# A four-layer graph network on one core: the second convolution's bias and node factor take another way

## The reference, cut to what matters

```python
def _L2_gnn_ref(H, A, mask, W, b):          # H = relu(layernorm(x)), the second norm of the kernel
    A_hat = A + jnp.eye(N, dtype=A.dtype)
    deg = A_hat.sum(axis=-1)
    dis = (deg + EPS) ** (-0.5)             # the node factor
    A_norm = dis[:, :, None] * A_hat * dis[:, None, :]
    H_lin = jnp.einsum('bni,oi->bno', H, W) + b
    out = jnp.einsum('bnm,bmo->bno', A_norm, H_lin)
    out = out * mask[:, :, None]
    return jax.nn.relu(out)
```

## Time and profile before

| | before |
|---|---|
| time, median of 3 runs (lowest to highest) | 666.03 us (664.73 to 666.15) |
| the profiled execution: its time, its span | 666.43 us, 664.5 us |
| TensorE matmul busy, share of the span | 621.7 us, 94% |
| ScalarE busy | 543.5 us, 82% |
| VectorE busy | 494.7 us, 74% |
| GpSimd busy | 380.8 us, 57% |
| granted TensorE clock, mean | 0.979 of full speed |
| TensorE's share of the chain that ended last | 86% |

### The profile page before, as it was taken

One profiled execution on the slowest core, in us unless ns is written; L12 is line 12 of the kernel. 1 busy time (PEld: TensorE's weight loads), 2 busy tenths in 40 slices (PEclk: granted clock), 3 DMA queues, 4 the chain that ended last, 5 costly groups with the idle time before them and its releaser, 6 DMA issues.

```text
span 664.5 us, 19876 instructions
## 1 busy us (share of the span) xinstructions
PE 621.7 (94%) x7220; PEld 495.6 (75%) x7220; DVE 494.7 (74%) x1530; ACT 543.5 (82%) x1271; POOL 380.8 (57%) x595
## 2 busy tenths in 40 slices
PE   4759999999999999999999999999999999999874
PEld 2545858788696978788696978788696978778563
DVE  4688786887778787878778687878777777975731
ACT  2877779898998989998998989998998889885334
POOL 3277453684847566475846566475846466636321
PEclk9988989999999999999999999999999999999977
DMA  9944590461908255380909154381908244300001
GB/s 117 253 93 134 70 198 3 96 114 31 193 4 157 69 127 98 82 142 27 199 3 164 62 132 94 85 139 31 194 3 150 96 117 41 97 2 18 16 1 33
DMA packets 171628, 61.24 MB, mean 92 GB/s; under 512 B 136641, under 2 KB 155146, under 8 KB 171530
## 3 DMA queue, kind: packets, MB, share of 16 engines
q1 hardware_dynamic: 170898, 59.73, 44.5%
q10 hardware_dynamic: 632, 0.22, 0.2%
HBM read 55.60 MB, written 4.33 MB: 90 GB/s over the span
## 4 chain that ended last, share of the span: by engine, by line
PE 86%; issue 4%; DVE 4%; ACT 2%; POOL 2%; DMA 1%; POOLq 0%; ACTq 0%; DVEq 0%
PE ps L1753 13%; PE ps L1789 9%; PE ps L1802 9%; PE ps L1909 8%; PE ps L1956 8%; PE ps L1739 7%; PE ps L1852 6%; PE ps L1849 5%; PE ps L1850 4%; PE ps L1939 4%; PE ps L1889 3%; PE ps L1695 2%; PE ps L1851 2%; PE ps L1776 1%; PE ps L1923 1%
## 5 line engine op out<-in xcount | busy, mean ns | idle before, releaser
L869 ACT ACTIVATE side<-d_all,sd 128x512 fp8e4<-128x512 f32 x256 | 163.3, 710 | 9.2 <-DVE pos L1302 6.3
L502 POOL TENSOR_TENSOR rstd<-ve,half_neg 128x4 f32<-128x4 f32 (+1 forms) x67 | 73.1, 1092 | 150.1 <-DVE ve L1384 60.7
L1753 PE MATMUL ps<-part,pos 128*128 128x66 bf16 x3072 | 102.5, 193 | 0.0
L1753 PEld LDWEIGHTS ps<-part,pos 128*128 128x128 fp8e4 x3072 | 99.4, 97 | 2.9 <-issue 0.7
L1365 DVE TENSOR_REDUCE best<-ps 128x128 f32<-128x896 f32 x64 | 69.5, 1086 | 27.6 <-PE ps L1853 27.5
L1302 DVE SCALAR_TENSOR_TENSOR pos<-side,edge 128x512 uint32<-128x512 uint32 x64 | 51.1, 798 | 29.0 <-ACT side L869 27.8
L1789 PE MATMUL ps<-adj_tr,h 128*128 128x512 f32 x128 | 60.6, 618 | 1.1 <-ACT h L775 1.1
L1956 PE MATMUL ps<-u,adj_tr 128*128 128x128 f32 x512 | 59.9, 275 | 0.7 <-ACT u L970 0.7
L1956 PEld LDWEIGHTS ps<-u,adj_tr 128*128 128x128 f32 x512 | 58.5, 192 | 1.4 <-ACT u L970 1.4
L1802 PE MATMUL ps<-adj_in,h 128*128 128x512 f32 x128 | 59.4, 608 | 0.0
L1739 PEld LDWEIGHTS ps<-part,edge 128*128 128x128 fp8e4 x1536 | 52.7, 99 | 8.5 <-issue 8.3
(11 more groups left out here) (164 smaller groups left out, 1468.9 us busy)
## 6 DMA issues: line engine op xcount, KB each, us to landing
adj_blk<-in_adj SPq DMA_DIRECT2D x64, 256.0 KB, 7.0
d_all<-d_dram SPq DMA_DIRECT2D x64, 256.0 KB, 5.1
adj_in<-in_adj SPq DMA_DIRECT2D x16, 1024.0 KB, 7.1
x_in<-in_x SPq DMA_DIRECT2D x16, 256.0 KB, 2.9
out_y<-y_out SPq DMA_DIRECT2D x15, 256.0 KB, 6.0
d_dram<-sd_t SPq DMA_DIRECT2D x64, 2.0 KB, 1.5
w_sb<-in_L_gnn_W SPq DMA_DIRECT2D x7, 64.0 KB, 2.1
b_sb<-in_L_gnn_b SPq DMA_DIRECT2D x1, 256.0 KB, 2.6
```

What stands on the lines that cost most here:

```text
L502: G.tensor_tensor(rstd[:, cut], ve[:, cut], half_neg[:, cut], ALU.pow).then_inc(power, 1)
L869: last = A.activation(side[:, t, :], d_all[:, h, :], ACT.Sign, bias=sd[:, 0, h, t:t + 1], scale=-1.0, saturate=False)
L1753: last = mm(ps[:, B_HEADS[q] + i // 2, o:o + VAL], pos[h % 2][:, t, i * P:(i + 1) * P], parts[n][:, t, h, :], start=False, stop=(i % 2 == ...
```

## The change

The bias product `conv_bias` and the making of `b2_rows` are gone. The node factor goes into the norm: VectorE multiplies the variance by the degree before GpSimd takes the power -1/2, so that `rstd2` and the offset hold the factor already and `h2` comes out scaled. `conv_linear` then gives `dis * H W`, and `conv_in`, which is now on VectorE and not on ScalarE, adds `dis * b` on the way out of PSUM. For the largest score, `smax_p` and `smax_t` are now whole: 128 columns and 128 rows, zero outside the 4 that are used, and the transpose and the product go over all 128.

```diff
@@ GpSimd, at the start
+            G.memset(smax_p[:], 0.0).then_inc(s_pool, 1)
+            G.memset(smax_t[:], 0.0).then_inc(s_pool, 1)
@@ GpSimd, degree_sums
                 if g.has(3):
                     pool.wait_ge(deg_ok, g.before(3).all(1))
+                    pool.wait_ge(bn2, g.before(3).all(3))
@@ ScalarE: the piece and its calls are gone
-            @of_graph
-            def conv_in(g):
-                act.wait_ge(lin2_ps, g.halves(1))
-                act.wait_ge(deg_out, g.whole(1))
-                if g.has(2):
-                    act.wait_ge(ay2_ps, g.before(2).all(1))
-                scaled(g, y2[g.two], bank(B_LIN).rearrange("p (t f) -> p t f", t=T), deg_pow[g.three][:, 0, :]).then_inc(y2_ok, 1)
@@ VectorE, top_score
-                V.tensor_reduce(smax_t[:], ps[0:HEADS, B_PROJ, 0:P], AX.X, ALU.min).then_inc(smaxt_ok, 1)
+                V.tensor_reduce(smax_t[0:HEADS, :], ps[0:HEADS, B_PROJ, 0:P], AX.X, ALU.min).then_inc(smaxt_ok, 1)
@@ VectorE, norm2, and the new piece
-                V.tensor_scalar(ve2[:, g.lo:g.hi], mv2[:, g.lo:g.hi, 1], LN_EPS, None, ALU.add).then_inc(bn2, 1)
+                dve.wait_ge(deg_in, g.whole(3))
+                V.scalar_tensor_tensor(ve2[:, g.lo:g.hi], mv2[:, g.lo:g.hi, 1], LN_EPS, deg[g.three][:, 0, g.lo:g.hi],
+                                       ALU.add, ALU.mult).then_inc(bn2, 1)
+            @of_graph
+            def conv_in(g):
+                dve.wait_ge(lin2_ps, g.halves(1))
+                dve.wait_ge(deg_out, g.whole(1))
+                if g.n == 0:
+                    dve.wait_ge(s_w0, 1)
+                if g.has(2):
+                    dve.wait_ge(ay2_ps, g.before(2).all(1))
+                for t in g.tiles:
+                    last = V.scalar_tensor_tensor(y2[g.two][:, t, :], bias_bc[:, 1, :], deg_pow[g.three][:, 0, t:t + 1],
+                                                  bank(B_LIN)[:, t * F:(t + 1) * F], ALU.mult, ALU.add)
+                last.then_inc(y2_ok, 1)
@@ VectorE, the loop (and likewise at the start and the end)
                 pair(1)(at(s - 4))
+                conv_in(at(s - 5))
                 attention(at(s - 4))
                 residual0(at(s - 4))
@@ TensorE
-                tr(ps[0:HEADS, B_PROJ, 0:P], smax_p[:], ident[:]).then_inc(smaxp_ps, 1)
+                tr(ps[:, B_PROJ, 0:P], smax_p[:], ident[:]).then_inc(smaxp_ps, 1)
...
-                mm(ps[:, B_PROJ + 1, 0:HEADS], smax_t[:, 0:1].broadcast_to([HEADS, P]), ident[0:HEADS, 0:HEADS],
+                mm(ps[:, B_PROJ + 1, 0:HEADS], smax_t[:, 0:1].broadcast_to([P, P]), ident[:, 0:HEADS],
                    start=True, stop=True).then_inc(smax_ps, 1)
...
             @of_graph
-            def conv_bias(g):
...
-                mm(bank(B_LIN), ones_b[:], b2_rows[:].unsqueeze(1).broadcast_to([P, T, F]), start=True, stop=False,
-                   skip_group_check=True)
...
             def conv_linear(g):
                 pe.wait_ge(h2t_sb, g.all(1))
...
+                if not g.later:
+                    if g.n >= 1:
+                        pe.wait_ge(u3_ok, g.before(1).halves(1))
+                        pe.wait_ge(z3_ok, g.before(1).halves(1))
+                    else:
+                        pe.wait_ge(best_ok, g.th(3, T))
                 for t in g.tiles:
-                    last = mm(bank(B_LIN)[:, t * F:(t + 1) * F], h2t[:, t * P:(t + 1) * P], w2_t[:], start=False,
-                              stop=(t == T - 1), skip_group_check=True)
+                    last = mm(bank(B_LIN)[:, t * F:(t + 1) * F], h2t[:, t * P:(t + 1) * P], w2_t[:], start=True, stop=True)
```

More of the change, by code:

```diff
@@ L121, in graph_kernel @@
         c6_bc = sb("c6_bc", [P, F])
-        b2_left = sb("b2_left", [P, F])
-        b2_parts = sb("b2_parts", [P, PARTS, F], bf16)
-        b2_rows = sb("b2_rows", [P, F], bf16)
         gamma_c = sb("gamma_c", [P, 1])
         beta_c = sb("beta_c", [P, 1])
-        ones_b = sb("ones_b", [P, P], bf16)
         b1_sb = sb("b1_sb", [P, T, F])
@@ L171, in graph_kernel @@
         d_all = sb("d_all", [P, HEADS, N])
-        smax_p = sb("smax_p", [P, HEADS])
-        smax_t = sb("smax_t", [HEADS, 1])
+        smax_p = sb("smax_p", [P, P])
+        smax_t = sb("smax_t", [P, 1])
         s_rel = sb("s_rel", [P, T, HEADS])
@@ L260, in graph_kernel @@
         s_units = sem("s_units")
-        s_b2 = sem("s_b2")
         s_w0 = sem("s_w0")
@@ L1031, in _ @@
             hidden0(at(3))
-            conv_in(at(0))
             row_sums(at(2))
@@ L1059, in _ @@
             projected(at(3))
-            conv_in(at(1))
             hidden1(at(2))
@@ L1088, in _ @@
                 projected(at(s - 3))
-                conv_in(at(s - 5))
                 row_sums(at(s - 3))
@@ L1114, in _ @@
             projected(at(15))
-            conv_in(at(13))
             sides(0)(at(15))
@@ L1136, in _ @@
             h2_transposed(at(14))
-            conv_in(at(14))
             hidden1(final(0))
@@ L1153, in _ @@
             h2_transposed(final(1))
-            conv_in(final(0))
-            conv_in(final(1))
             conv_relu(final(0))
@@ L1173, in _ @@
             V = nc.vector
[L1175 to L1190, removed]
             V.memset(ones_row[:], 1.0).then_inc(s_setup, 1)
@@ L1194, in _ @@
             V.memset(shift_c[:], SHIFT)
-            V.memset(ones_b[:], 1.0)
             for i in range(2):
@@ L1253, in scores @@
                 V.transpose(sd_t[:], sd[:].rearrange("p k h t -> p (k h t)")).then_inc(dt_ok, 1)
-                V.tensor_reduce(smax_p[:], sd[:, 0, :, :], AX.X, ALU.min).then_inc(smaxp_ok, 1)
+                if g.n == 0:
+                    dve.wait_ge(s_pool, 5)
+                V.tensor_reduce(smax_p[:, 0:HEADS], sd[:, 0, :, :], AX.X, ALU.min).then_inc(smaxp_ok, 1)
             @of_graph
@@ L1469, in unit_columns @@
                 V.tensor_copy(ident_b[:], ident[:]).then_inc(s_units, 1)
-            def bias_rows():
-                three_rows(bias_bc[:, 1, :], b2_parts, b2_left, b2_rows, s_b2)
             norm0(at(0))
@@ L1502, in _ @@
             edge_marks(at(1))
-            bias_rows()
             part_rest(at(1))
@@ L1517, in _ @@
             pair(1)(at(1))
+            conv_in(at(0))
             scores(at(2))
@@ L1543, in _ @@
             pair(1)(at(2))
+            conv_in(at(1))
             attention(at(2))
@@ L1597, in _ @@
             pair(1)(at(14))
+            conv_in(at(13))
             attention(at(14))
@@ L1622, in _ @@
             pair(1)(at(15))
+            conv_in(at(14))
             attention(final(0))
@@ L1641, in _ @@
             norm2(final(1))
+            conv_in(final(0))
+            conv_in(final(1))
             residual2(final(0))
@@ L1996, in _ @@
             mean_value(at(2))
-            conv_bias(at(0))
             conv_linear(at(0))
@@ L2020, in _ @@
             h2_transposed(at(1))
-            conv_bias(at(1))
             row_sums(at(2))
@@ L2049, in _ @@
             for s in range(7, GRAPHS + DEPTH - 1 - 7):
-                conv_bias(at(s - 5))
                 conv_linear(at(s - 5))
@@ L2075, in _ @@
                 h0_transposed(at(s - 1))
-            conv_bias(at(13))
             conv_linear(at(13))
@@ L2097, in _ @@
             h2_transposed(at(14))
-            conv_bias(at(14))
             conv_linear(at(14))
@@ L2116, in _ @@
             h2_transposed(final(1))
-            conv_bias(at(15))
             conv_linear(final(0))
```

## The result

The changed kernel takes 671.37 us, median of 7 runs (667.41 to 672.29), against 666.03 us (664.4 to 667.67, 7 runs): a ratio of 1.0078, 95% interval 1.0055 to 1.0102. It is slower by 5.3 us, where 4.05 were forecast (670.1 us); the time lies inside the forecast's own range of 668 to 672 us. Its profiled execution took 671.91 us with a span of 670.1, 5.6 more than the span of before, at a mean granted clock of 0.972 (0.979 before).

What follows compares the result with a forecast made beforehand. TensorE was taken to set the pace, other engines costing time only where it waits. Terms 2.2 + 0.75 + 0.8 - 0.2 + 0.6 - 0.1 = +4.05 us gave 670.1 us; own range 668 to 672, 8-in-10 range 665.4 to 673.2.

Steps and rivals of the forecast that it cites:

- The direction and the mechanism: Slower, chance 0.73: conv_in on VectorE waits for conv_linear, delaying the chain to h1 until TensorE waits for it.
- The loop: Eleven passes: h1 comes late to TensorE's transposes, +0.20 us per pass, +2.2 us in all.
- The tile: Largest score's product as a whole tile: -0.18 us per graph where h1 is not waited for.
- h1 comes in time: Rival, chance 0.15: a 0.4 us shorter chain to h1 gives -2 us in the loop; 666 us, no change.
- The bias product, the bias rows, ScalarE's relief: Per graph: removed product and row-making were hidden by waits, and y's earlier finish is used by nobody: gain 0.
- TensorE's relief counts: Rival, chance 0.11: h2t ready 0.4 us earlier at conv_linear, so TensorE's savings count: at most 658 us, half 663.
- Graph 1: At the start, conv_in ahead of the attention delays x and the transposes of h1: +0.75 us.
- it costs more: Rival, chance 0.16: longer start wait lowers TensorE's clock again, and conv_in is held up beside GpSimd's xf: 673 us.
- Graph 2: At the start, rden moves by 1.89 us and h1 ends after TensorE wants it: +0.8 us.
- Graph 14: Near the end, h1 stands behind other ScalarE work, so only the whole tile's gain counts: -0.2 us.
- Graph 15: Near the end, a shift of 1.9 us against h1's slack of 1.3: +0.6 us.
- The very end: Last stretch: the bias product has less cover and y is as quick on VectorE: -0.1 us.

Runs made afterwards that it cites:

- e1: The changed kernel with conv_in one piece later everywhere, behind the attention product and ahead of the residual: 662.59 us, ratio 0.9958 to the kernel before.
- e7: The changed kernel with conv_in behind the attention everywhere and the largest score's small 4-column, 4-row products restored: 666.5 us, ratio 1.001 to the kernel before.
- e8: The changed kernel with conv_in as one 512-column instruction in the same place, using the first tile's node factor for all four: 665.13 us, ratio 0.9988.
- e4: The changed kernel with the largest score's products over 4 columns and 4 rows again: 669.65 us, ratio 1.0071 to the kernel before.
- e3: The kernel before without the bias product, the bias left out of the result and its rows still made: 665.56 us, ratio 1.0009.
- e6: The changed kernel with conv_in moved behind the attention at the start and the end alone: 669.31 us, ratio 1.0051 to the kernel before.
- e5: The changed kernel with conv_in moved behind the attention in the loop alone: 666.03 us, ratio 1.0002 to the kernel before.
- e2: The kernel before with only the largest score's two products over whole tiles: 662.2 us, ratio 0.9948.

## Why the prediction was right, and the terms that were not

*The direction and the mechanism.* The chain was forecast step by step, and each link was found: VectorE idle for 0.86 us (0.8 forecast), the four instructions at 1.12 (1.06), a new wait at h1 and at no other place in the loop, `conv_linear` still waiting for `h2t` (the weight loads for 0.47 us, where 0.5 or more was named). e1, e7 and e8 show that nothing else lengthens the pass. x was forecast 3.29 behind the start of `conv_linear` and came 3.24 behind it; the transposes of h1 8.85, and came 8.81.

*The loop: +1.6 for a forecast of +2.2.* The forecast was 0.20 us per pass, measured 0.15 over 11. The tile, mis-sized with 0.18 instead of 0.28, does not matter here (e4), and would have mattered in every case in which h1 is in time: "h1 comes in time" had -2 for the loop and measures 11 x 0.28 = -3.1 (e1).

*The bias product, the bias rows, ScalarE's relief: 0.* Right: e3 shows it for the product, and e7 for all three together. The rival in which TensorE's relief counts fails at the point that it named: `conv_linear` starts no closer to the transposes ahead of it.

*Graph 1: +1.7 for +0.75.* The mechanism was right: `att` and `x` took 0.69 each and not 1.20 and 1.64. After, VectorE:

```profile
78.85 1.12 DVE L1364 SCALAR_TENSOR_TENSOR y<-bias_bc,deg_pow,ps 128x128 f32<-128x128 f32 x4 [1.07 <-PE ps L1868]
...
80.59 0.69 DVE L1306 TENSOR_TENSOR att<-num,rden 128x512 f32<-128x512 f32 x1
81.31 0.69 DVE L1316 TENSOR_TENSOR x<-att,xf 128x512 f32<-128x512 f32 x1
```

and TensorE, which answers to the earlier trace rows:

```profile
77.66 1.16 PE L1868 MATMUL ps<-w_t,h2t 128*128 128x128 f32 x8 [0.45 <-ACT h2t L923]
...
86.88 1.12 PE L1761 MATMUL ps<-ident,h 128*128 128x128 f32 x4 [2.86 <-ACT h L773]
...
88.08 6.18 PE L1787 MATMUL ps<-adj_in,h 128*128 128x512 f32 x8
```

The transposes start 9.22 us behind `conv_linear` instead of 86.66 - 78.13 = 8.53: +0.69, as forecast. The other 1.0 us is what the prediction had put into its rival "it costs more": the transposes themselves take 1.12 us instead of 0.66 and the product behind them 6.18 instead of 5.40. Three microseconds of that product after (window, its length, then busy time of PE, PEld, DVE, ACT, POOL, granted clock, DMA share, GB/s):

```profile
88.00:91.00 3.00, 3.00 (x6) 1.45 (x6) 2.24 (x8) 2.97 (x9) 0.85 (x1) 0.50 1.18 266
```

The transposes and the product in e1, and the same three microseconds there:

```profile
86.02 0.66 PE L1761 MATMUL ps<-ident,h 128*128 128x128 f32 x4 [1.52 <-ACT h L773]
86.92 3.68 PE L1787 MATMUL ps<-adj_in,h 128*128 128x512 f32 x8
```

```profile
88.00:91.00 3.00, 3.00 (x9) 1.32 (x8) 2.67 (x12) 3.00 (x8) 2.17 (x2) 1.00 1.30 163
```

After a wait of 2.86 us TensorE runs at a granted clock of 0.50 (1.2 GHz); in e1, after 1.52, at 1.00 (2.4 GHz). The length of the wait alone does not decide this: before and in e3, it fell after 1.47 us, and in e8, after 2.64, the product took 4.79 us, between the two.

*Graph 2: +0.2 for +0.8.* h1 was waited for, as forecast, but the transposes moved by 0.42 us against `conv_linear` (127.70 - 118.59 = 9.11, before 8.69). The step that was missing is x's wait for GpSimd's `xf`, which the prediction had counted in the loop and not here. VectorE and GpSimd before, then VectorE after:

```profile
119.42 0.69 DVE L1349 TENSOR_TENSOR x<-att,xf 128x512 f32<-128x512 f32 x1 [0.26 <-issue]
```

```profile
118.27 1.06 POOL L623 TENSOR_TENSOR xf<-xe,xb 128x256 f32<-128x256 f32 x1
```

```profile
120.82 0.24 DVE L1302 RECIPROCAL rden<-den 128x16 f32<-128x16 f32 x1
...
122.13 0.69 DVE L1316 TENSOR_TENSOR x<-att,xf 128x512 f32<-128x512 f32 x1
```

Against `conv_linear`, `rden` came 1.86 us later, as forecast (1.89), but x only 1.48: before, VectorE had been idle for 0.26 us ahead of it and had started it behind the end of `xf`, at 119.33 (the trace names this wait `issue`, so its cause is read from the times). Further, the tile gave 0.28 back: its product stands behind h1's transposes here (e4 against the changed kernel: 38.44 against 38.15).

*Graph 14: +0.5 for -0.2, the step that had its sign wrong.* "h1 stands behind other ScalarE work of that pass" held before, where ScalarE started h1 without a wait, and no longer holds. ScalarE and TensorE before:

```profile
572.84 1.63 ACT L775 ACTIVATE h<-x,off,rstd 128x128 f32<-128x128 f32 x4
```

```profile
574.15 0.38 PE L1714 MATMUL ps<-ident,smax_t 4*128 4x4 f32 x2
574.53 3.70 PE L1789 MATMUL ps<-adj_tr,h 128*128 128x512 f32 x8
```

and after:

```profile
576.38 1.65 ACT L773 ACTIVATE h<-x,off,rstd 128x128 f32<-128x128 f32 x4 [0.59 <-POOL off L502]
```

```profile
577.10 0.28 PE L1699 MATMUL ps<-ident,smax_t 128*128 128x4 f32 x2
578.08 3.70 PE L1774 MATMUL ps<-adj_tr,h 128*128 128x512 f32 x8 [0.70 <-ACT h L773]
```

h1 was ready at 574.47 and TensorE wanted it at 574.53: no slack at all, where I had not looked for the row. In e1, `attention(14)` ahead of `conv_in(13)`, the stretch is 37.06.

*Graph 15: +0.65 for +0.6.* Right. e8, with 0.37 us less work, has all of it back (30.81), e1 and e6 half (31.17 and 31.16).

*The very end: +1.4 for -0.1, and not shown to be the change's.* The last stretch from the mark of graph 15, before, after, e6 and e3:

```profile
633.85:664.50 30.65, 19.24 (x117) 16.93 (x116) 8.96 (x37) 11.51 (x30) 5.09 (x9) 0.78 0.06 18
```

```profile
638.06:670.10 32.04, 21.81 (x116) 19.60 (x116) 10.08 (x41) 10.40 (x26) 5.10 (x9) 0.68 0.06 17
```

```profile
635.75:664.80 29.05, 17.84 (x116) 16.18 (x116) 10.09 (x41) 10.20 (x26) 5.09 (x9) 0.86 0.06 19
```

```profile
635.22:667.50 32.28, 22.15 (x116) 20.07 (x116) 9.10 (x37) 11.54 (x30) 4.93 (x9) 0.69 0.06 17
```

With 116 matmuls (117 before, with the bias product) the stretch takes 32.0 to 32.3 us at a clock of 0.68 or 0.69, 30.65 at 0.78, and 29.05 at 0.86. e3 has the order of before and is the longest of all; e4 has the order of the changed kernel, and with 29.14 one of the shortest, while e8, in the same order, takes 32.11. So this stretch goes by the clock of the execution, and with one trace of each kernel no part of it can be put down to the change. The runs of the changed kernel go with their clock too, from 667.41 us at a mean of 0.984 to 672.29 at 0.974. That leaves 5.6 - 1.4 = 4.2 us of the change in these two traces, against 4.05 forecast: in part by luck, with graph 1's clock (+1.0) and graph 14 (+0.7) under, graph 2 and the loop (-1.2) and the lead of 0.5 at the first mark over. The loop and graph 15, which came near their forecasts, are 2.3 of the 4.2 us; the rest agrees because the misses cancel.

*What stays open.* Whether the clock's share of the start comes in each run: two of the traces with the changed kernel's start (e4, e5) have 40.99 and 40.95 us there, but why a wait of 1.47 us was followed by the low clock before and in e3, and one of 1.44 to 1.53 in e1, e2, e6 and e7 was not, no run here tells.

## What to carry to other kernels

Work that is moved to an engine with time to spare costs what it delays there, and that is set by its place in the engine's order and its length together, against the slack of what stands behind it: ahead of the attention 1.1 us of work with a wait in front made the kernel 0.8% slower, one piece later the same work was free (e7), and in the first place 0.75 us of work was nearly free too in the loop (e8). Look, for each engine's order, for the waits that are there already, and put new work into the one that its input has arrived for. And take parts of a change apart before judging it: here one detail, whole tiles for a 4-row product, held all the gain (0.5%), and the late h1 hid it.

## What was not expected of the hardware

- A product over 4 rows and 4 columns between full 128-row tiles costs 0.28 us more than the same over 128 rows with zeros, spread over three starts: its own (0.31 against 0.23), the next (0.31 against 0.14), and the one after (0.50 against 0.47). The Trainium skill, "TensorEngine Tiling (Array Packing)", section Key Properties, has changes of tiling mode drain the engine; the direction agrees (e2, e7), and the page gives no size. That a drain is the cause is not shown: only the shape was changed.
- Four VectorE instructions of 128 columns that read PSUM, an SBUF tile and a scalar took 1.12 us, one of 512 columns 0.75: about 0.12 us for each instruction more (0.37 over three).
- `conv_in` was not seen slowed beside GpSimd. In the start GpSimd's large addition runs from 79.23, while `conv_in` runs from 78.85 to 79.97; `att` and x took 1.20 and 1.64 at this time before. All its instructions of the changed kernel (shortest, median and longest in ns):

```profile
L1364 DVE SCALAR_TENSOR_TENSOR y<-bias_bc,deg_pow,ps x64: 339/342/349, 78.9 to 640.0; 128x128 f32<-128x128 f32 x64
```

The Trainium skill, "GPSIMD Engine Reference", section Specifications, names instructions with two SBUF inputs for such contention; `conv_in` has one SBUF tensor, and by that rule, the trace agrees.
